# Two-layer decoder with routed experts on one core: the first expert stage begins on 40 full tiles while the last 16 row scatters are still to be made, and rotary-stage work changes engines

## The reference, cut to what matters

```python
x = layernorm(x + taylor_attention(x))              # layer 0, 8 heads, 2nd order Taylor features
x = layernorm(x + cross_attention(x, ctx))          # 16 heads of 64, 77 context tokens ("wide")
x = layernorm(x + gelu_experts(x))                  # 8 experts 128->512->128, best 2 of 8 by softmax
x = layernorm(x + causal_attention(x))              # layer 1, 16 heads of 8, ALiBi
x = layernorm(x + rotary_cross_attention(x, ctx))   # 16 heads of 8, rms-normalised q and k, rotated
x = layernorm(x + swiglu_experts(x) + shared_mlp(x))# 8 experts 128->256->128, best 2 of 8

# an expert layer, for each token: two experts e with gates g
out = sum(g[e] * mlp_e(x) for e in top2(router(x)))
# rotary: q and k are divided by the root of their mean square per head (1/sqrt), then turned by cos/sin tables
```

## Time and profile before

| what | value |
|---|---|
| median of 3 runs | 3029.79 us (3029.34 to 3032.92) |
| the profiled execution | 3032.73 us |
| its span (first to last instruction) | 3030.9 us |
| granted TensorE clock, mean | 0.964 |
| busy: TensorE / VectorE / ScalarE / GpSimd | 2741.7 / 1885.3 / 2042.3 / 1380.0 us |
| wide stage, from its first rows to its last scores | about 228 to 1090 us |
| first gelu tile to last gelu tile | about 1157 to 1428 us |
| causal, rotary stage | about 1488 to 2020, 2060 to 2624 us |
| swiglu stage | from 2656 us |

### The profile page before, as it was taken

One profiled execution on the slowest core, in us unless ns is written; L12 is line 12 of the kernel. 1 busy time (PEld: TensorE's weight loads), 2 busy tenths in 40 slices (PEclk: granted clock), 3 DMA queues, 4 the chain that ended last, 5 costly groups with the idle time before them and its releaser, 6 DMA issues. The chain is left out here.

```text
span 3030.9 us, 69270 instructions
## 1 busy us (share of the span) xinstructions
PE 2741.7 (90%) x21504; PEld 1984.9 (65%) x21504; DVE 1885.3 (62%) x5517; ACT 2042.3 (67%) x7107; POOL 1380.0 (46%) x1882
## 2 busy tenths in 40 slices
PE   8999999999999957998799999978999999699886
PEld 6766777777777746997355555546666666457774
DVE  6883343444444444554688888877888888544555
ACT  6767777777778733443799999967877878522224
POOL 3442224444444454554433333324466666624665
PEclk9999999999999978999899999988999999899998
DMA  9910030320400402222210000000000000001225
GB/s 263 338 44 15 29 109 13 94 64 20 137 17 20 135 30 73 71 73 79 86 57 8 10 9 10 10 24 7 16 24 28 27 28 21 29 26 56 79 80 182
DMA packets 179959, 185.07 MB, mean 61 GB/s; under 512 B 32844, under 2 KB 168537, under 8 KB 179216
## 3 DMA queue, kind: packets, MB, share of 16 engines
q1 hardware_dynamic: 162032, 145.14, 16.1%
q0 software_dynamic: 17280, 34.13, 3.3%
q10 hardware_dynamic: 288, 1.38, 0.1%
HBM read 58.34 MB, written 111.48 MB: 56 GB/s over the span
## 5 line engine op out<-in xcount | busy, mean ns | idle before, releaser
L1376 DVE TENSOR_REDUCE wide_neg_max<-banks 128x4 f32<-128x308 f32 x256 | 122.5, 479 | 474.3 <-PE banks L970 449.6
L678 POOL TENSOR_TENSOR wide_probs<-wide_exps,wide_inv_sum 128x308 f32<-128x308 f32 x256 | 179.0, 699 | 489.1 <-DVE wide_inv_sum L1385 485.9
L1104 ACT ACTIVATE causal_exps<-causal_biased,causal_neg_max 128x128 f32<-128x128 f32 x1024 | 325.9, 391 | 31.2 <-DVE causal_neg_max L1376 29.6
L1107 ACT ACTIVATE wide_exps<-banks,wide_neg_max 128x77 f32<-128x77 f32 x1024 | 315.2, 326 | 0.3 <-DVE wide_neg_max L1376 0.2
L658 POOL DMA_INDIRECT sorted_x<-send,place_i x240 | 242.2, 1009 | 97.7 <-ACT send L1067 55.3
L1104 ACT ACTIVATE rotary_exps<-banks,rotary_neg_max 128x77 f32<-128x77 f32 x1024 | 247.6, 335 | 43.6 <-DVE rotary_neg_max L1376 42.6
L1091 ACT ACTIVATE wide_probsT<-banks 77x512 f32<-77x512 f32 x256 | 151.8, 593 | 154.1 <-PE banks L979 149.9
L1639 ACT ACTIVATE gelu_hidden<-banks,gelu_slot 128x256 f32<-128x256 f32 x284 | 116.6, 470 | 156.0 <-PE banks L1816 151.8
L1107 ACT ACTIVATION_READ_ACCUMULATOR wide_exps<-banks,wide_neg_max 128x1 f32 x1024 | 213.9, 209 | 0.0
L1570 POOL DMA_INDIRECT results<-swiglu_tile_out,swiglu_dest_i x142 | 146.6, 1032 | 144.0 <-DVE swiglu_tile_out L1721 101.5
L616 POOL TENSOR_TENSOR rotary_keys<-rotary_kT,rest 128x308 f32<-128x308 f32 x256 | 184.2, 740 | 57.2 <-ACT rotary_kT L791 54.4
(11 more groups left out here) (382 smaller groups left out, 7295.1 us busy)
## 6 DMA issues: line engine op xcount, KB each, us to landing
sorted_x<-blank SPq DMA_DIRECT2D x1, 34848.0 KB, 116.8
sorted_x<-blank SPq DMA_DIRECT2D x4, 8712.0 KB, 30.3
gelu_tile_in<-sorted_x SPq DMA_DIRECT2D x71, 132.0 KB
swiglu_tile_in<-sorted_x SPq DMA_DIRECT2D x71, 132.0 KB
gelu_back<-results SPq DMA_DIRECT2D x16, 512.0 KB, 8.2
swiglu_back<-results SPq DMA_DIRECT2D x16, 512.0 KB, 5.6
X<-in_x SPq DMA_DIRECT2D x8, 512.0 KB, 7.3
regions<-in_g_w SPq DMA_DIRECT2D x2, 2048.0 KB, 20.9
```

Of the source, the lines that this page charges most:

```text
L678: pool.tensor_tensor(probs[:, m % SLOTS], exps[:, m % SLOTS], inv_sum[:, m % SLOTS].unsqueeze(2).to_broadcast([P, HU, NK]), ALU.mult).then ...
L1104: last = act.activation(exps[:, (NU * c.c + k) % ES, h], scores[:, h * NK:(h + 1) * NK], ACT.Exp, bias=neg_max[:, k % SLOTS, h:h + 1])
L1107: last = act.activation(exps[:, k % SLOTS, h], scores[:, h * NK:(h + 1) * NK], ACT.Exp, bias=neg_max[:, k % SLOTS, h:h + 1], accum_out=exp ...
L1376: dve.tensor_reduce(neg_max[:, k % SLOTS], scores.rearrange("p (h n) -> p h n", h=HU), AX.X, ALU.max, negate=True).then_inc(max_done, 1)
```

## The change

1. **First expert stage.** Wide no longer scatters its last 8 sequences. `sending` leaves them out, and the gelu stage makes those 16 scatters itself: GpSimd puts one in front of its wait for tile t at t = 2, 4, ..., 32; ScalarE fills `send` twice at t = 0 and once at t = 4, 8, 12, 16, 20 and 24, **in front of** that tile's gelu. The table is made twice: before the first tile for N1 = 40 tiles that the first 56 sequences fill completely (from a copy of the counts, `base_early`), and again by 17 small operations, one per tile at t = 4 to 20, for the other 31. SyncE's first loads wait for 56 sequences' scatters instead of 64's, and those from tile 40 on for all. NT stays 71.
2. Both expert stages: the output ring YR goes from 4 to 6 tiles, and the tile numbers are copied from PSUM once.
3. **Rotary.** The two normalisations per pair and `scaled` go from VectorE to GpSimd, the four `sums` copies per pair go from VectorE to ScalarE (after the slot's exps). Two waits are added on VectorE for what GpSimd now reads or writes.

```diff
@@ sending
-                if pair is not None and pair.c % 4 == 3 and not (kind == "rotary" and pair.c == n_pairs - 1):
+                if pair is not None and pair.c % 4 == 3:
                     slot = 8 * n + k - (19 if late else 18)
-                    if slot >= 0 and slot % 2 == 0 and slot // 2 < 16:
+                    if slot >= 0 and slot % 2 == 0 and slot // 2 < 16 and 2 * pair.c - 6 + slot // 4 < n_seq - route["left"]:
@@ rotary, GpSimd's step
+                    if n is not None and kind == "rotary" and k in (3, 4):
+                        s, b = n.c % 4, k - 3
+                        pool.wait_ge(rstd_done, n.count(1, 1))
+                        pool.tensor_scalar(X[:, n.index(2, b), :], z[:, s, b], mean_var[:, s, b, 0:1], rstd[:, s, b:b + 1],
+                                           ALU.subtract, ALU.mult).then_inc(x_written, 1)
+                    if f is not None and kind == "rotary" and k == 0:
+                        pool.wait_ge(halves_done, f.count(1, 1))
+                        pool.wait_ge(qk_rstd_done, ROOT * (f.c // 2 + 1))
...
+                        pool.tensor_tensor(scaled[:].rearrange("p n h d -> p (n h) d"), rotated[:, f.c % QK],
+                                           qk_rstd[:, f.c // 2 % 2, f.c % 2].unsqueeze(2).to_broadcast([P, 4 * H, 8]), ALU.mult).then_inc(scaled_done, 1)
@@ rotary, ScalarE's step
+                    at = lagged(c, u, k, OLAG)
+                    if kind == "rotary" and at is not None and at[1] % 2 == 1:
...
+                        act.activation(sums[:, b, j * P:(j + 2) * P], o_bank[(m // 2) % 2][:, 0:2 * P], ACT.Copy).then_inc(o_done, 1)
@@ VectorE's added waits
+                if j >= 2:
+                    dve.wait_ge(scaled_done, 2 * j - 2)
...
+                    if u.c >= 4:
+                        dve.wait_ge(x_written, 2 * (u.c - 3))
@@ experts
-    XR, YR, WR, BR, ZR = 6, 4, 3, 8, 5
+    LAST = S - 8
+    N1 = 0 if swiglu else min(40, (2 * LAST * P - E * (TS - 1)) // TS)
+    XR, YR, WR, BR, ZR = 6, 6, 3, 8, 5
@@ experts, SyncE
-                sp.wait_ge(done, all_scattered)
+                sp.wait_ge(done, all_scattered if swiglu else scattered_already + 16 * 2 * (LAST // SEND))
...
+                if t == N1 and not swiglu:
+                    for done in scattered:
+                        sp.wait_ge(done, all_scattered)
+                    sp.wait_ge(table_done, 2)
@@ experts, GpSimd
+            def scatter(n, which):
+                pool.wait_ge(send_done, n + 1)
+                pool.indirect_dma_start(sorted_x, ..., send[:, n % SEND, which, :], None).then_inc(scattered[n % SEND], 16)
...
             for t in range(NT):
+                if not swiglu and 2 <= t < 34 and t % 2 == 0:
+                    scatter((t - 2) // 4, (t - 2) // 2 % 2)
                 pool.wait_ge(y_done, t + 1)
@@ experts, ScalarE, gelu branch
+                    if t == 0:
+                        for n in range(SEND):
+                            fill(n)
+                    elif t % 4 == 0 and SEND <= t // 4 + 1 < 8:
+                        fill(t // 4 + 1)
                     if t >= 2:
                         act.wait_ge(y_ps, t - 1)
@@ experts, VectorE
+                if not swiglu and 4 <= t < 21:
+                    rest_of_table(t - 4)
+                if t + 2 == N1 and not swiglu:
+                    dve.wait_ge(table_done, 2)
```

More of the change, by code:

```diff
@@ L1275, in put @@
                                            route["base"].unsqueeze(2).to_broadcast([P, E, B]), ALU.add))
+                    if route["base_early"] is not None and b == n_seq // B - 1:
+                        link(dve.tensor_copy(route["base_early"], route["base"]))
                     dve.tensor_tensor(route["base"], route["base"], count_bank, ALU.add).then_inc(base_done, 1)
@@ L1357, in step @@
                         take_logits(r)
-                    if n is not None and k in ((4, 5) if late else (3, 4)):
+                    if n is not None and kind != "rotary" and k in ((4, 5) if late else (3, 4)):
                         s, b = n.c % 4, k - (4 if late else 3)
@@ L1386, in step @@
                     at = lagged(c, u, k, OLAG)
-                    if at is not None and at[1] % 2 == 1:
+                    if kind != "rotary" and at is not None and at[1] % 2 == 1:
                         pair, m = at
@@ L1436, in step @@
                         divide(u, (k - 4) // 2)
[L1437 to L1443, removed]
                     if u is not None and not late and k == Z_AT:
@@ L1478, in experts @@
         row_f, row_i = sb("row_f", [1, NT]), sb("row_i", [1, NT], I32)
+        numbers, taken = sb("numbers", [1, NT]), sb("taken", [P, E])
         slot = sb("slot", [P, WR, W])
@@ L1659, in link, with count_tiles @@
                 dve.wait_ge(routed, links[0])
+            begin = cum[:, 1, E - 1:2 * E]
+            def count_tiles(n, ends, rounding):
+                if n == 0:
+                    link(dve.tensor_tensor(count_f[:], ends, region[:], ALU.subtract))
+                elif n == 1:
+                    link(dve.tensor_scalar(count_i[:], count_f[:], float(rounding), None, ALU.add))
+                else:
+                    link(dve.tensor_scalar(tiles_i[:], count_i[:], TS.bit_length() - 1, None, ALU.logical_shift_right))
@@ L1661, in _ @@
             link(dve.tensor_scalar(region[:], consts["rank8"], -float(CAPACITY), float(E * CAPACITY), ALU.mult, ALU.add))
-            link(dve.tensor_tensor(count_f[:], w["base"], region[:], ALU.subtract))
-            link(dve.tensor_scalar(count_i[:], count_f[:], float(TS - 1), None, ALU.add))
-            link(dve.tensor_scalar(tiles_i[:], count_i[:], TS.bit_length() - 1, None, ALU.logical_shift_right))
+            for n in range(3):
+                count_tiles(n, w["base"] if swiglu else w["base_early"], TS - 1 if swiglu else 0)
@@ L1673, in _ @@
[L1673 to L1678 removed]
+            link(dve.tensor_copy(numbers[:], ids[0:1]))
@@ L1679, in _ @@
+            for n in range(7):
+                write_table(n, 0, NT if swiglu else N1)
+            if not swiglu:
+                link(dve.tensor_scalar(taken[:], begin[:, 0:E], -1.0, float(N1), ALU.mult, ALU.add))
+                link(dve.tensor_scalar(taken[:], taken[:], 0.0, None, ALU.max))
+                link(dve.tensor_tensor(taken[:], taken[:], tiles_i[:], ALU.min))
             dve.wait_ge(table_done, 1)
```

88 lines of the change are left out of this document (63 added, 25 removed).

## The result

The change makes the kernel slower: 3071.35 us (median of 4 runs, 3067.95 to 3073.06) against 3031.18 us for the kernel before on the same chip (4 runs, 3029.34 to 3032.92). The ratio is 1.013, with a 95% interval of 1.0115 to 1.0145. The forecast was 3039, +9.2 us, with 3064 as its upper end; measured are +40.2. The direction was right, and 31 us are missing. The profiled execution took 3072.12 us with a span of 3070.3, 39.4 longer than the span of before.

What follows compares the result with a forecast made beforehand. It took TensorE to bound the gelu loop, lost time before it, and VectorE to pace rotary's middle. Terms -23.0 + 42.6 + 12.6 - 23 = +9.2 on the median 3029.8 gave 3039 us, range 3010 to 3064.

Steps and rivals of the forecast that it cites:

- The order of queues on ScalarE: Gelu loop: each of six fills waits ahead of gelu, stalling TensorE 7.1 us (+42.6), plus 2.1 for the clock (+12.6).
- fills are hidden: Rival for the gelu loop: ScalarE is somehow not held, both stall terms go, 2984 us; chance 0.12.
- Against it: the order of the queues: Gelu loop: objection to hidden fills, since ScalarE waits for a chain beginning after the point where it should work.
- the edits at nothing: Gelu loop and expert stages: later table operations, GpSimd's scatters (3.2 us average per 3.73 us tile) and YR = 6 cost nothing.
- The meeting: Between wide and gelu: engines meet 2.3 us after the last scatter, not the 9.4 seen later; wide ends 22.0 us earlier.
- -15 for the start: End of wide: gain in place of -22.0 us if the engines' meeting takes the longer 9.4 us.
- The first table: Ahead of gelu: four operations over 360 instead of 639 elements, one new copy of about 0.2; -1.0 us.
- Rotary: Rotary's middle: the pair falls from 18.04 to 17.0 us, 22 x 1.04 = -23 us; bounds -36 and +5.
- there VectorE sets the pace: Rotary's middle, stretch at 2390.6: VectorE busy 16.68 of 17.4 us, TensorE 14.64; VectorE costs at most 1.64 per pair.
- TensorE's floor: Rotary: 16.4 us per pair, read from pairs before routing, as the least TensorE allows; those pairs gain nothing.
- rotary brings nothing: Rival for rotary: GpSimd's longer queue blocks VectorE or comes late with keys, 3062 us; chance 0.15.
- YR = 6: Both expert stages: more output buffers bring nothing, as the output-ring wait lasted 21 ns in each of 134 instances.

Runs made afterwards that it cites:

- the twelfth run: Changed kernel with the six late fills two tiles later, plus two indirect DMAs ending wide and four ending rotary: 3011.16 us against 3031.61 for the kernel before.
- the seventh run: Changed kernel with the six late fills two tiles later and four output buffers instead of six: 2979.74 us, -25.7 against the kernel before.

## Why the prediction was wrong

*The order of queues on ScalarE* was right, and so was its price: 7.1 + 2.1 = 9.2 us per fill was forecast, and 8.7 measured, on both kinds of chip (52.2 and 52.7 us for six). Moving the fill by one tile and by two took off what the chain says. The rival "fills are hidden" is out; with them truly hidden the kernel is 22 to 26 us faster than before on prompt chips, and not the 46 of that rival, for the reasons below.

*"Against it: the order of the queues" left one thing out of the sum.* The gelu loop costs 14 us more on the late chips while scatters go between the result DMAs, holes or none. The prediction put "The scatters bring GpSimd from 2.56 to 3.84 us in every second tile of 3.73 [...] so it catches up" among the edits at nothing. On the prompt chips that step is right. On the chip of the prediction it is the step that failed, and the largest miss: +13.9. What the runs show in its place: on a late chip the completion of matmuls reaches VectorE up to 2.3 us late in tiles 3 to 35, while the scatters go out, and TensorE waits. That it is the scatters rests on where the loss ends (tile 36, behind the last scatter at t = 32, while in the twelfth run the fills end at t = 26 and the table at t = 20); no run took them out on a late chip, and why they and late completions go together stays open.

*The meeting* failed next: "Nothing in the trace tells me why; I take the first" took 2.3 us where the earlier trace rows showed 9.4, and it was 9.5. The bound for it (-15 for the start) stood in the text, and was the value. Behind gelu the drain lengthened by 4.4, which the prediction didn't name at all; together 11.6. The experiments show what the drain takes in each case, not why. The first table gave its 1 us. Another 1.9 us of the start are the wide stage's own, whose end came that much later in this execution.

*Rotary* brought 15.3 and not 23. The step that failed is "there VectorE sets the pace", with the sum over three moves. The stretch that it was read from is the extreme of a pattern of four; the one just before it in the kernel before has TensorE at 17.22 of 17.4:

```profile
2373.20:2390.60 17.40, 17.22 (x157) 12.47 (x156) 15.74 (x41) 15.03 (x56) 12.74 (x16) 1.00 0.10 29
```

The normalisation alone brings all of it, and 71 of the 115 us that left VectorE bring nothing. On GpSimd it takes 0.80 us, where the sum had 0.3 to 0.6. Pairs before routing gained a little (16.0 and not 16.4), so 16.4 wasn't TensorE's floor either; with TensorE busy for 442.6 of 465 us, what is left to gain in the middle is 5%. The rival "rotary brings nothing" is out as a whole, and right for two parts of three. By the shared port that the Trainium skill names (Perfetto Trace Analysis, section Optimizing Scalar/DVE Operations), a move to GpSimd might not help; here the one move that helped was to GpSimd, where the operation takes 0.80 us against a mean of 0.82 on VectorE in the earlier trace rows, and the other one to GpSimd, `scaled`, brought nothing. The rule says "might", and these runs don't contradict the port, only its use as a forecast.

*YR = 6* brought nothing, shown by the seventh run; the 3.4 us of the swiglu loop on the first chip are not the ring's, since its wait is 21 ns on both sides, and on prompt chips the loop is 197.1 with either ring.

The sum of the misses: 9.6 at the start, -3.0 in the stalls, +13.9 in the ordinary tiles, +5.4 behind gelu, +7.7 in rotary, -3.4 elsewhere are 30.2, and 9.2 + 30.2 = 39.4.

## What to carry to other kernels

Before a wait is put ahead of work on an engine, walk from what it waits for back to that engine: if the chain begins behind the work queued after the wait, the wait is a stall that no idle share of the engine hides; here it was gone with two tiles of distance. An engine's busy share says that it is loaded, not that it sets the pace; try single operations one at a time before three are moved. Count instances in the trace before a theory is built on their number: two scatters too few made a count that fits look refuted. And where two instances of the same step in the trace differ by 7 us with no reason to be seen, the dear one belongs in the sum until the reason is known.

## What the runs showed of the hardware

- The same program runs 26 to 30 us slower on the chips of the prediction and of the twelfth run than on the five others. As much as that lies in the swiglu loop, where other engines wait for TensorE's completion tile by tile: 197.1 us on the one kind, 224 to 228 on the other, while the causal loop takes 503 us on both and the changed rotary 517.4 and 517.5. On the late ones another engine was seen to start 2.16 us (swiglu) and 2.34 us (gelu) after the recorded end of the matmul that it waited for, on prompt ones 0.04 and 0.11 to 0.14.
- GpSimd's drain at the end of wide and rotary took 12.2 to 12.4 us behind 112 indirect DMAs, 13.7 behind 113, and 3.5 to 5.4 behind 114 to 128, but 12.2 behind 116 of which four were issued early; it agreed to 0.2 us in the two programs that were profiled twice. Two DMAs of no use at the end, 2.5 us of issue, made it shorter by 8.7.
- Holes of 3.0 to 3.3 us in TensorE's work were followed by the lower clock in five cases of six, for 3.4 us at 1.2 GHz. With holes of 6.7 us the lower clock lasted 6.8 us, of which 2.7 to 3.8 lay in the hole itself.
